# Putting the expert stage of a perceiver kernel into the hand-written order of its two streams, and one slot's masked copies on ScalarE

## The reference, cut to what matters

```python
x = x + xattn_ref(layernorm(x), ctx)     # causal self-attention, attention over 257 keys, feed-forward
x = x + attn_ref(layernorm(x))           # 2 layers: a delta-rule recurrence (8 heads), then a gated MLP; rmsnorm
x = x + ffn_ref(layernorm(x))            # mixture of 32 experts plus a shared one
```

```python
scores = sigmoid(h @ gate_w.T); sc = scores + gate_bias
# of 8 groups of 4 experts keep the 4 whose two best add up highest; of those experts keep the best 8
tkw = scores[top8] / sum(scores[top8]) * 2.5         # combine[t, e]: this weight, or 0
routed = sum_e combine[t, e] * (silu(h @ w_gate[e].T) * (h @ w_up[e].T)) @ w_down[e].T
shared = (silu(h @ sh_gate.T) * (h @ sh_up.T)) @ sh_down.T
out = x + routed + shared
```

## Time and profile before

| | |
|---|---|
| median of 3 runs | 866.61 us (863.3 to 868.63) |
| the profiled execution | 867.67 us; span 865.9 us, so 1.8 us lie around it |
| TensorE | 667.7 us busy (77%), 6,704 matmuls |
| VectorE | 490.9 us busy (57%), 1,180 instructions |
| ScalarE | 239.0 us busy (28%), 529 instructions |
| GpSimd | 94.3 us busy (11%), 127 instructions |
| mean granted TensorE clock | 0.805 of full speed |
| chain that ended last | PE 63%, DVE 22%, DMA 3%, ACT 3%, POOL 3%, issue 3% |

### The profile page before, as it was taken

How to read it: one execution, slowest core, us unless ns; L and a number is a source line. 1 busy time by engine, 2 the same in 40 slices (tenths; PEclk the granted TensorE clock), 3 DMA queues, 4 the chain that set the end, 5 groups by cost and what they waited for, 6 DMA issues and landing times.

```text
span 865.9 us, 16141 instructions
## 1 busy us (share of the span) xinstructions
PE 667.7 (77%) x6704; PEld 449.1 (52%) x6704; DVE 490.9 (57%) x1180; ACT 239.0 (28%) x529; POOL 94.3 (11%) x127
## 2 busy tenths in 40 slices
PE   2448376336569999998699599999569998689995
PEld 1225243214568887776388589866324443334442
DVE  4472854447695583575837944645665545754443
ACT  1112123027323124355154103244221222222221
POOL 1324225133000001101010000102200000100000
PEclk9568666758565699987899855999679999679998
DMA  9990000310000000000000000040000000100001
GB/s 353 296 377 1 24 0 0 58 16 0 2 2 2 2 3 3 1 2 2 1 2 2 2 3 2 2 156 1 0 0 0 1 0 4 22 0 0 0 0 24
DMA packets 13309, 29.53 MB, mean 34 GB/s; under 512 B 2272, under 2 KB 7008, under 8 KB 12992
## 3 DMA queue, kind: packets, MB, share of 16 engines
q1 hardware_dynamic: 13248, 28.64, 10.3%
HBM read 26.54 MB, written 2.10 MB: 33 GB/s over the span
## 4 chain that ended last, share of the span: by engine, by line
PE 63%; DVE 22%; DMA 3%; ACT 3%; POOL 3%; issue 3%; SPq 2%; DVEq 0%; POOLq 0%; ACTq 0%
PE psum L687 7%; PE psum L688 6%; PE psum L697 6%; PE psum L505 4%; PE psum L539 4%; PE psum L630 3%; PE psum L665 3%; PE psum L619 3%; POOL rstd L899 2%; PE psum L525 2%; DMA zlast<-in_ctx_last 2%; PE psum L612 2%; PE psum L546 2%; PE psum L485 2%; PE psum L566 2%
## 5 line engine op out<-in xcount | busy, mean ns | idle before, releaser
L1319 DVE TENSOR_TENSOR mid<-psum,act_o 128x512 f32<-128x512 f32 x64 | 44.3, 692 | 90.1 <-PE psum L697 82.1
L410 PE MATMUL psum<-ident,yn 128*128 128x128 f32 x96 | 21.5, 376 | 76.5 <-DVE yn L979 46.2
L687 PE MATMUL psum<-yT,weg_sb 128*128 128x512 f32 x136 | 75.9, 641 | 5.8 <-DVE arena L1313 5.7
L880 ACT ACTIVATE act_o<-psum 128x512 f32<-128x512 f32 x64 | 38.2, 597 | 137.9 <-PE psum L690 137.9
L688 PE MATMUL psum<-yT,weu_sb 128*128 128x512 f32 x136 | 73.2, 621 | 0.0
L697 PE MATMUL psum<-mid,wed_sb 128*128 128x512 f32 x136 | 69.3, 595 | 4.0 <-DVE mid L1288 2.5
L410 PEld LDWEIGHTS psum<-ident,yn 128*128 128x128 f32 x96 | 15.2, 191 | 82.1 <-DVE yn L979 50.8
L730 ACT ACTIVATE arena<-psum 128x512 f32<-128x512 f32 (+1 forms) x60 | 35.5, 599 | 79.6 <-PE psum L505 37.7
L505 PE MATMUL psum<-arena 32*64 32x128 f32 x1024 | 45.3, 345 | 8.0 <-ACT arena L730 3.6
L687 PEld LDWEIGHTS psum<-yT,weg_sb 128*128 128x128 f32 x136 | 27.2, 205 | 39.7 <-issue 31.2
L899 POOL TENSOR_TENSOR rstd<-ve,neg_half 128x4 f32<-128x4 f32 x44 | 46.5, 1058 | 3.4
(11 more groups left out here) (232 smaller groups left out, 1277.5 us busy)
## 6 DMA issues: line engine op xcount, KB each, us to landing
arena<-in_ctx_t SPq DMA_DIRECT2D x16, 514.0 KB, 7.7
arena<-in_ctx_z SPq DMA_DIRECT2D x16, 512.0 KB, 8.9
XA<-in_x SPq DMA_DIRECT2D x1, 1024.0 KB, 4.9
zlast<-in_ctx_last SPq DMA_DIRECT2D x4, 256.0 KB, 16.9
x_mid<-XA SPq DMA_DIRECT2D x2, 512.0 KB, 2.6
X<-x_mid SPq DMA_DIRECT2D x8, 128.0 KB, 4.7
weg_sb<-in_we_gate SPq DMA_DIRECT2D x2, 512.0 KB, 6.4
weu_sb<-in_we_up SPq DMA_DIRECT2D x2, 512.0 KB, 7.3
```

The lines of the kernel that those rows point to most:

```text
L410: last = pe.transpose(bank[:, jj * D:(jj + 1) * D], src[u][:, jj, :], ident[:, :])
L687: pe.matmul(banks[4 * u][:, :], weg_sb[:, w, :], yT[u][:, :], start=True, stop=True)
L880: act.activation(act_g[u][:, :], banks[4 * u][:, :], ACT.Silu).then_inc(x_silu, 1)
L1319: dve.tensor_tensor(act_gu[u][:, :], banks[4 * u + 1][:, :], act_g[u][:, :], ALU.mult).then_inc(x_gu, 1)
```

## The change

**The expert section becomes stages of the two streams.** Its loop is gone. `ROUTE` names seven routing stages (`eln`, `etr`, `elog`, `ro0`, `ro1`, `ro2`, `ec`); behind them each stream has, for slot h = 0 and then slot 1, the stages `xh` (shared expert, then 16 pairs), `endh` (last down and copy) and `backh` (transposes, add, output DMAs). `TURNS` grows from 156 to 246 letters, and its first part changes a little too.

- Stream A routes while stream B is in the last steps of its second layer, from `p3` to `down`. Stream B routes between the units of A's slot 0. In A's last MLP the order moves as well: `mtr` to `down` and `fin` of A now come before `o` of B.
- One slot per stream is at work at a time, with the stream's four banks: gate, up, spread, accumulator. A unit's matmuls are gate, up, spread, then down of the stream's previous unit. The matmuls signal one by one: gate waits for the silu of the unit before, up for the first product (L1319 before, L1316 now), spread and down for the second (L1322 before, L1320 now).
- The selection is cut into three stages of VectorE work: `ro0`, `ro1`, `ro2`. Its tiles lie in the arena, once per stream.
- In `ec` ScalarE copies a slot's weights out of PSUM, waits for VectorE's split, copies the middle part, and only then takes the next slot.
- SyncE loads the expert weights after stream A's `o` of layer 1.

**Masked copies.** In `lout` both slots' four copies are on ScalarE; VectorE has none.

The diff, cut to its core:

```diff
+ROUTE = ["eln", "etr", "elog", "ro0", "ro1", "ro2", "ec"]
-TURNS = ("AABAAABABBAABBABAAAAABABAABABABABBAABABAAAAAABBBAABAAABBBAABABABABABAABAABAABAABABABAABBAABAABAB"
...
+TURNS = ("AABAAABABABABBABAAABAABBAABABABABABBABAABAAAAAABAABABABBBBABAABAABABABBAAABABABABABABABAABAABAA"
...
+    stages += [(kind, 0) for kind in ROUTE]
+    for h in range(NU):
+        stages += [(f"x{h}", p) for p in range(-1, NPAIR)] + [(f"end{h}", 0)]
+    stages.insert(stages.index(("x1", -1)) + 1, ("back0", 0))
+    stages.append(("back1", 0))
...
-            sp.wait_ge(s_omm[NU - 1], 2 * L)
-            sp.wait_ge(s_omm[0], 2 * L)
+            for k in range(NU):
+                sp.wait_ge(s_omm[k], 2 * L - 1)
...
+                    elif kind in ("x0", "x1") and u == int(kind[1]):
+                        p, n = l, nth(kind, l)
+                        x0, x1, x2, x3 = (banks[4 * pr + k] for k in range(4))
+                        w = p % (NPAIR + 1)
+                        if n == 0:
+                            pe.wait_ge(e_cf, (pr + 1) * NU)
+                        else:
+                            pe.wait_ge(x_silu[pr], n)
...
+                        pe.matmul(x0, weg_sb[:, w, :], yT[g][:, :], start=True, stop=True).then_inc(x_gate[pr], 1)
+                        if p < 1 and n > 0:
+                            pe.wait_ge(x_a[pr], n)
+                        elif n > 0:
+                            pe.wait_ge(x_gu[pr], routed(n))
+                        pe.matmul(x1, weu_sb[:, w, :], yT[g][:, :], start=True, stop=True).then_inc(x_up[pr], 1)
+                        if p >= 0:
...
+                            pe.wait_ge(x_a[pr], n)
+                            pe.matmul(x2, spread[:, p * P:(p + 1) * P], c3[g], start=True, stop=True).then_inc(x_comb[pr], 1)
...
+                            pe.matmul(x3, wed_sb[:, (p - 1) % (NPAIR + 1), :], act_a[pr], start=(p == 0), stop=False,
+                                      skip_group_check=True).then_inc(x_down[pr], 1)
...
-                    elif kind == "lout" and u == 0:
+                    elif kind == "lout":
                         act.wait_ge(l_omm[u], pi + 1)
...
+                    elif kind == "ec":
+                        act.wait_ge(e_ctr, g + 1)
+                        copy(cf[g], b0[0:E, :]).then_inc(e_cf, 1)
+                        act.wait_ge(e_c3, g + 1)
+                        copy(c3[g][E:2 * E, :], cmid[g]).then_inc(e_mid, 1)
...
-                    elif kind == "lout" and u == 1:
-                        dve.wait_ge(l_omm[u], pi + 1)
...
+                    elif kind in ("x0", "x1") and u == int(kind[1]):
+                        p, n = l, nth(kind, l)
+                        dve.wait_ge(x_silu[pr], n + 1)
+                        dve.wait_ge(x_up[pr], n + 1)
...
+                            dve.wait_ge(x_a[pr], n)
+                            dve.tensor_tensor(act_gu[pr], banks[4 * pr + 1], act_g[pr], ALU.mult).then_inc(x_gu[pr], 1)
+                            dve.wait_ge(x_gu[pr], routed(n + 1))
+                            dve.wait_ge(x_comb[pr], routed(n + 1))
+                            dve.wait_ge(x_down[pr], n)
+                            dve.tensor_tensor(act_a[pr], banks[4 * pr + 2], act_gu[pr], ALU.mult).then_inc(x_a[pr], 1)
```

More of the change, by code:

```diff
@@ L332, in system, with nth, routed @@
             return divmod(n, H)
+        def nth(kind, p):
+            return int(kind[1]) * (NPAIR + 1) + p + 1
+        def routed(n):
+            return n - (n + NPAIR) // (NPAIR + 1)
         def chunks_of(pr, u):
@@ L390, in _ @@
                     sp.dma_start(dst[:, cols_, :], src[:, cols_, :]).then_inc(experts_in[c], 16)
-            for it in range(IT):
-                for u in range(NU):
-                    g = it * NU + u
-                    need(sp, e_xo, it, u)
+            for kind, l, pr in STEPS:
+                if kind[:4] == "back":
+                    h = int(kind[4])
+                    g = pr * NU + h
+                    sp.wait_ge(e_xo[pr], h + 1)
                     for a in range(NA):
@@ L400, in _ @@
                             sp.dma_start(out[s0:s0 + 2 * GT - 1:2, :].rearrange("t (j d) -> j t d", d=D),
-                                         r[u][p0:p0 + NJ, :, :]).then_inc(out_done[u], 16)
-            for u in range(NU):
-                sp.wait_ge(out_done[u], 16 * (IT * 8 + 1))
+                                         yn[g][p0:p0 + NJ, :, :]).then_inc(out_done, 16)
+            sp.wait_ge(out_done, 16 * NG * 8)
         @block.tensor
@@ L955, in _ @@
                         rsqrt(st, g, ss[g][:, 0:GT], GT, eps_rms, f_rr)
+                    elif kind == "eln":
+                        pool.wait_ge(e_var, g + 1)
+                        rsqrt(st, g, mv[g][:, :, 1], GT, eps_ln, e_rstd)
             st.end()
-            with pool.Fori(0, IT) as it:
-                st = Steps(pool, pool_steps)
-                for u in range(NU):
-                    need(pool, e_var, it, u)
-                    rsqrt(st, u, mv[u][:, :, 1], GT, eps_ln, e_rstd)
-                st.end()
         @block.vector
@@ L1128, in _ @@
                     continue
+                if kind == "eln":
+                    for u in range(NU):
+                        g = pr * NU + u
+                        stats(st, lambda jj: gcols(X, g)[:, jj * D:(jj + 1) * D], g, e_var)
+                if kind[:2] == "ro":
+                    if kind == "ro0":
+                        dve.wait_ge(e_sig, (pr + 1) * NU)
+                    choose(st, pr, int(kind[2]))
+                    continue
                 if kind == "onorm":
@@ L1203, in _ @@
                             last.then_inc(l_inv, 1)
-                    elif kind == "lout" and u == 1:
-                        dve.wait_ge(l_omm[u], pi + 1)
-                        lanes = b1.rearrange("p (m n) -> p n m", m=C16)
-                        for j in range(NC):
-                            last = dve.tensor_scalar(TT[g].rearrange("p (n c) -> p n c", c=T)[:, :, j * C16:(j + 1) * C16],
-                                                     lanes, chunk[j], None, ALU.mult)
-                        last.then_inc(l_out[u], 1)
                     elif kind in ("s1", "s2", "s3"):
```

320 lines of the change are left out of this document (138 added, 182 removed).

## The result

The changed kernel takes 839.21 us (median of 4 runs, 836.87 to 843.55) against 866.34 us (4 runs of the kernel before, one more than in the table above); the ratio is 0.9695, with a 95% interval from 0.9644 to 0.9746. The forecast was 844 us, in a range from 825 to 861. The profiled execution took 836.87 us with a span of 835.1 us.

What follows compares the result with a forecast made beforehand. TensorE was taken to bound the units, VectorE-led serial chains about 40 us ahead of each iteration. B's `o` at 585.7, first unit 627.2, TensorE's list 813.9, routing 827.6, tail 839.6, clock +4: span 843.6, forecast 844 us, range 825 to 861.

Steps and rivals of the forecast that it cites:

- case 1: Whole kernel: the time comes out as computed, 836 to 852 us; chance 45%.
- A's `o` starts: Attention section up to A's `o`: no change expected, start at 499.3 us as before.
- from there to the end of B's `o`: A's MLP (16.8 us) and 3.1 us lost to `fin` now come ahead, so B's `o` ends at 585.7, not 565.8.
- to the end of A's first routed unit: After B's `o`: A's routing beside B's norm and MLP, 41.5 us, ending at 627.2 before the clock's addition.
- to the last unit's down: Expert section: TensorE's remaining list up to 813.9, plus 13.7 us for B's routing, giving 827.6 before the clock's addition.
- tail: From the last unit's down to the end: 12.0 us instead of 13.0, set by issuing the output DMAs.
- the attention order: Attention section's changed order: counted at 0, between -10 (VectorE freed, slow stretch shortened) and +11 (`lout` and `ah` slow).
- case 2: A's projection ends the slow stretch early, B's routing gaps are swallowed: 828 us, B's `o` ending before 575; chance 20%.
- Case 3: Attention section, layer 1: less cover for A's solve, `lout` and `ah` at 1.2 GHz cost 11: 855 us; chance 20%.
- a block of length D costs D - 2.1: B's routing between A's units: VectorE's strict list makes each block cost its length less 2.1 us, 13.7 us together.
- Case 4: Expert units: one slot doesn't keep TensorE busy, 0.5 us lost a unit over some 30 units: 859 us; chance 8%.
- Case 5: A's slot 0 at 1.2 GHz, 16 units +45, so 888 us; other reading, a 2 us restart per block; chance 7%.

Runs made afterwards that it cites:

- experiment 5: Kernel before with only the attention section's stages in the changed kernel's order, old expert loop and masked copies kept: 872.01 us, ratio 1.0077.
- experiment 6: Kernel before with the changed kernel's attention order and A's closing residual (fin.1A) behind B's last copy of the solve (p3.1B): 862.15 us, ratio 0.9952.
- experiment 11: Changed kernel without the six extra matmuls on a constant in A's otr of layer 1: 847.01 us, ratio 0.9771.
- Experiment 3: Changed kernel with fin, LayerNorm, selection and ec cut into finer pieces, one behind each of A's units: 828.82 us, ratio 0.9588.
- experiment 7: Kernel before with only slot 1's masked copies moved to ScalarE: 870.61 us, ratio 1.0062.
- experiment 8: Changed kernel with stream A's seven routing stages moved back behind B's last down: 864.18 us, ratio 0.9996.
- experiment 1: Changed kernel with stream A's fin moved behind stream B's p3 of layer 1: 831.43 us, ratio 0.9606.

## Why the prediction was right, and where its steps were off

The changed kernel is 5 us below the forecast, and case 1 ("as computed", 836 to 852) holds it. The mechanism was right too: the two chains are hidden, VectorE's list sets what each block of B's routing costs, and the cost comes out within 0.2 us for `fin`, `ro0` and `ro1`, and within 0.9 at worst. Other terms came out by luck, as shown below. The steps, as times of the span:

| step | predicted | in the profile of after |
|---|---|---|
| A's `o` starts | 499.3, as before | 487.5 |
| from there to the end of B's `o` | 66.5 + 19.9 = 86.4 | 86.6 |
| to the end of A's first routed unit | 41.5, and 2 for the clock | 44.1 |
| to the last unit's down | 186.7 + 13.7, and 2 for the clock | 204.7 |
| tail | 12.0 | 12.2 |
| end | 843.6 | 835.1 |

**The start.** 11.8 us were gained ahead of A's `o`, where the sum had 0. 4.2 of them are not the change's: the first section, whose code is the same, ended that much earlier in this profile. The stretch behind it is 7.6 us shorter (306.0 instead of 313.5), with the same 3,948 matmuls: TensorE is busy 5.6 us less in it (252.9 instead of 258.5, at a granted clock of 0.82 instead of 0.80) and idle 2.0 us less. The order of the attention section does it: with the old expert stage and the old masked copies the stretch is 305.7 us long in experiment 5 and 306.7 in experiment 6. The bounds of -10 to +11 for the attention order held this term, and the value 0 was the wrong choice in it.

**B's `o`.** The term of 19.9 us agrees to 0.2, by two errors of opposite sign. The wait ahead of `o` was 3.91 instead of 3.1; that much was right. Not in the sum was what it did to the clock: 14 us at 0.51, some 6 us. The other way, the slow stretch behind A's `o` was shorter. TensorE's timeline of the changed kernel:

```profile
510.95 2.74 PE L560 MATMUL psum<-spread 96*128 96x512 bf16 x6
513.49 1.91 PE L424 MATMUL psum<-ident,yn 128*128 128x128 f32 x8
515.32 2.29 PE L657 MATMUL psum<-wo_sb,yT 128*128 128x128 f32 x16
```

And a stretch of it, with the granted clock behind GpSimd's column:

```profile
515.00:517.00 2.00, 2.00 (x14) 1.68 (x13) 0.24 (x1) 0.96 (x2) 0.00 (x0) 0.79 0.00 0
```

Six extra matmuls, transposes and A's projection (L560, L424, L657) now stand between `lout` and `ah`, the clock rises during them, near 516, and the 256 small matmuls of B's `ah` behind them take 7.65 us. In the kernel before they took 13.84, and the clock rose only near 545:

```profile
522.20 13.84 PE L539 MATMUL psum<-mid,arena 64*64 64x32 f32 x256
...
544.12 1.59 PE L410 MATMUL psum<-ident,yn 128*128 128x128 f32 x8
```

That is 6.2 us back, and experiment 11 gives them away again by its one edit. So case 2 happened in part: the slow stretch ends at A's projection, which gave back 6 us and not 12 (and, by experiment 11, not by the projection alone), while B's gaps were not swallowed. Its marker, `o` of B ending before 575, was met with 574.1, but by the 11.8 us gained ahead of A's `o`; it says nothing for case 2.

Case 3 happened in part as well, earlier than it is looked for in this row. Its mechanism was 1.2 GHz through A's `lout` and `ah` of layer 1. TensorE's timeline of `ah` in the changed kernel, and in the kernel before:

```profile
433.76 13.75 PE L553 MATMUL psum<-wed_sb,arena 64*64 64x32 f32 x256 [0.65 <-ACT arena L739]
```
```profile
451.07 7.65 PE L539 MATMUL psum<-wed_sb,arena 64*64 64x32 f32 x256
```

`lout` ran at 2.4 GHz (3.92 us), `ah` at 1.2. All kernels here with the new attention order show this (13.64 to 13.76 us, behind a wait of 0.65 or 0.66); the two with the old order don't (7.65 and 7.66, without a wait). The stretch up to A's `o` became 7.6 us shorter in spite of these 6.1 us. In front of B's `o` another 10 us were lost to `fin`'s wait and its clock, of which the forecast had the wait (3.1) and not the clock.

In this row the sum was right about what both make together, +6 and -6. A reader should not take its agreement for a proof of its working.

**To the first unit.** 44.1 against 43.5. The 6.86 us wait ahead of B's MLP and its slow first pairs came as forecast.

**B's routing.** The rule "a block of length D costs D - 2.1" was the core of the forecast, and this is the row-by-row comparison:

| block | predicted us | wait of TensorE |
|---|---|---|
| `fin` | 2.8 | 2.70 |
| `eln` | 2.9 | 1.79 + 0.59 |
| `ro0` | 0.9 | 0.72 |
| `ro1` | 3.2 | 3.31 |
| `ro2` | 0.4 | about 0.15 |
| `ec` | 3.5 | 1.04 + 1.63 |
| sum | 13.7 | 11.9 |

VectorE's timeline shows the longest of them. Behind A's second product come the ten instructions of `ro1`, and A's next first product starts 5.4 us after the last one ended, though its matmuls were done long before:

```profile
652.00 0.69 DVE L1320 TENSOR_TENSOR arena<-psum,arena 128x512 f32<-128x512 f32 x1 [0.43 <-PE psum L721]
652.61 0.68 DVE L1008 TENSOR_TENSOR arena<-arena,before 128x512 f32<-128x512 f32 x1
...
658.08 0.69 DVE L1316 TENSOR_TENSOR arena<-psum,arena 128x512 f32<-128x512 f32 x1
```

5.4 - 2.1 is 3.3, the wait of 3.31 us. Experiment 3 confirms the rule by its other end: pieces of about 2.1 us cost 0.17 to 0.60. By the rule that VectorE and ScalarE are strict FIFO (the Trainium skill, TensorE: Matmul & The Clock Gate, The HAM clock gate) no ready product overtakes a waiting row, and the trace agrees with its 3.31 us. The stretch as a whole took 2.3 us more than predicted, though the waits were 1.8 less. Of the 4 us that this leaves, two are clock: behind the waits of 2.70 and 3.31 TensorE ran at 1.2 GHz for 3.7 us each time (up pairs of 1.75 and 1.73, down pairs of 1.91 us), at some 1.8 us, and the sum had that once. The other 2 are not placed. (In the forecast's list of TensorE's rows, 202 x 0.86 + 64 x 0.22 is 187.8, not 187.5.)

**The tail** was 12.2: the DMAs are issued from 826.06 on, in 3.59 and 3.70 us, as in the earlier trace rows.

**The rivals.** Case 4 did not happen: from 680 on TensorE is busy without a hole, and the units follow each other at 2.80 us. Case 5 neither: the granted clock is 0.95 from 612 to 680. What it names occurs, but costs 2 us behind each of the two longest waits and not a whole slot; a restart behind each of the six blocks, the case's other reading, would have made six.

## What to carry to other kernels

When a second stream's work is hidden between the units of a saturated engine, the partner's list is what counts: cut its blocks to the slack of the loop (here 2.1 us), and count each block above the slack as its length less the slack. Look for short work that now stands ahead of something TensorE waits for; with six products moved behind one copy, the kernel won 7.8 us, twice what the wait itself had cost, because the clock came back with it. Work moved to a less busy engine can do the same harm there (experiment 7). And where a term's two bounds are 20 us apart, the agreement of the total says little about the term.

## What the runs showed of the hardware

- **A wait of 3.9 us brought the clock down, in front of small matmuls that did not bring it back.** The 256 matmuls of `o` are 64 rows by 32 columns; TensorE was busy 13.70 of 14.00 us with them and stayed at 0.51. The kernel before shows the same on a longer stretch: 24.00 of 24.00 us busy at 0.50. Eight extra 512-column matmuls (3.60 us) between small ones did not raise it in either kernel; six of them (2.74 us) with eight transposes and the 16 matmuls of the projection directly behind did. Without the six, the transposes and the projection did not (experiment 11).
- **The length of a wait alone doesn't say what it costs.** In front of 512-column pairs the wait of 2.70 us cost 3.7 us at 1.2 GHz in the changed kernel; the same wait in experiment 8 cost nothing more, and the pair behind it ran at full speed:

```profile
651.66 1.12 PE L712 MATMUL psum<-yT,weu_sb 128*128 128x512 f32 x2 [2.70 <-DVE arena L1316]
```

  Waits of 0.4 to 1.8 us between units had no cost beyond themselves (pairs of 1.02 to 1.13 us behind them). But ahead of A's `ah` the clock fell behind a wait of 0.65 us, and 13.75 us of small matmuls ran at 1.2 GHz. Whether the wait or what stood ahead of it decided there isn't separated.
- **Small matmuls ran at either clock, and it also fell while they ran.** The 256 of B's `ah` ran at 2.4 GHz throughout, 7.65 us, right behind the projection, and B's `o` at 3.92 and 3.90 us where no wait stood ahead of it (experiments 1 and 6). A's `o` in the changed kernel began at 2.4 GHz behind a wait of 1.66 us and fell to 1.2 GHz after about 1 us, with TensorE busy all the time:

```profile
487.49 6.20 PE L644 MATMUL psum<-arena,weg_sb 64*64 64x32 f32 x128 [1.66 <-DVE arena L1268]
```
```profile
487.49:488.50 1.01, 1.01 (x34) 1.01 (x36) 0.98 (x3) 0.00 (x0) 0.00 (x0) 1.00 0.00 0
488.50:489.50 1.00, 1.00 (x26) 1.00 (x25) 0.93 (x3) 0.00 (x0) 0.00 (x0) 0.52 0.09 16
```

  So the same rows cost double or not by what stood ahead of them.
- **The same code differs by some 6 us between profiles.** The first section, whose instructions are the same in all kernels here, ended at 185.77 in the profile before, at 181.52 in that of the changed kernel, and between 180.42 and 186.66 in the others. A single profile can't place a difference of this size unless it is counted from the end of that section.
